# Graph attention on one core: GpSimd waits for the landing of one pair's gathers before it issues the next pair's

## The reference

```
q, k, v = x @ Wq + bq, x @ Wk + bk, x @ Wv + bv          # per node
e       = edge_attr @ We                                 # per edge
alpha   = sum_d(q[dst] * (k[src] + e)) / sqrt(16)        # per edge and head
attn    = softmax of alpha over the edges of one dst
out     = segment_sum(attn * (v[src] + e), dst)
x_r     = x @ Wskip + bskip
beta    = sigmoid([out, x_r, out - x_r] @ Wbeta)
out     = beta * x_r + (1 - beta) * out
out     = x + relu(layernorm(out) * gamma + beta_ln)
result  = layernorm(x + out)
```

## Time and profile before

| | |
|---|---|
| runs: median (lowest to highest) | 2126.05 us (2125.98 to 2133.83), 3 runs |
| profiled execution: span, first to last instruction | 2774.7 us |
| PE matmul busy in it | 2009.6 us, 72% |
| DVE busy | 1801.8 us, 65% |
| GpSimd busy | 1497.6 us, 54%, of it 1568 gathers 1483.1 us |
| ACT busy | 1140.6 us, 41% |
| DMA moved | 468.47 MB, GpSimd's queue 206.24 MB |
| mean granted TensorE clock | 0.77 |

### The profile page before, as it was taken

How to read it: one execution, slowest core, us unless ns; L and a number is a source line. 1 busy time by engine, 2 the same in 40 slices (tenths; PEclk the granted TensorE clock), 3 DMA queues, 4 the chain that set the end, 5 groups by cost and what they waited for, 6 DMA issues and landing times.

```text
span 2774.7 us, 45026 instructions
## 1 busy us (share of the span) xinstructions
PE 2009.6 (72%) x11492; PEld 1805.8 (65%) x11492; DVE 1801.8 (65%) x4040; ACT 1140.6 (41%) x3750; POOL 1497.6 (54%) x1591
## 2 busy tenths in 40 slices
PE   7478888888776577667766767757687777778775
PEld 5467777777666566566665767656576667667664
DVE  7465565566666566566665667657676676777764
ACT  0133333344343344344443444434454454454455
POOL 0555555555556555565555555555555555555531
PEclk9677777777777777777777777778788777777786
DMA  8556666666655555555554655555565555555541
GB/s 308 185 165 184 176 184 183 178 180 180 172 167 167 158 159 167 154 174 165 167 167 143 176 163 167 175 149 165 164 176 167 170 176 168 169 172 180 169 123 39
DMA packets 298585, 468.47 MB, mean 169 GB/s; under 512 B 49862, under 2 KB 193034, under 8 KB 298230
## 3 DMA queue, kind: packets, MB, share of 16 engines
q1 hardware_dynamic: 222680, 259.30, 31.3%
q0 software_dynamic: 75648, 206.24, 26.2%
HBM read 414.62 MB, written 50.73 MB: 168 GB/s over the span
## 4 chain that ended last, share of the span: by engine, by line
PE 54%; issue 17%; another core or an unknown queue 13%; ACT 8%; DVE 3%; DMA 2%; ACTq 1%; POOL 0%; SPq 0%; POOLq 0%; DVEq 0%
PE sum_ps L928 18%; PE q_ps L825 12%; PE e_ps L812 10%; ACT dist_en L1046 3%; PE max_ps L841 2%; PE sum_ps L866 2%; PE sum_ps L865 2%; PE sum_ps L851 2%; PE max_ps L834 2%; PE sum_ps L850 2%; ACT hot_en L1055 1%; PE sum_ps L894 1%; PE sum_ps L895 1%; DMA xt_buf<-xT 1%
## 5 line engine op out<-in xcount | busy, mean ns | idle before, releaser
L706 POOL DMA_INDIRECT kv<-kv_tab,src_all x1568 | 1483.1, 946 | 1144.6 <-DVE kve L1373 683.8
L1373 DVE TENSOR_TENSOR kve<-kv,e_ps 128x1024 f32<-128x1024 f32 x392 | 462.2, 1218 | 756.0 <-issue 626.2
L928 PE MATMUL sum_ps<-wv,hot_en 128*128 128x136 f32 x3136 | 683.7, 394 | 15.0 <-issue 11.4
L928 PEld LDWEIGHTS sum_ps<-wv,hot_en 128*128 128x128 f32 x3136 | 626.1, 291 | 60.4 <-issue 58.5
L825 PE MATMUL q_ps<-q_win,hot_ne 128*128 128x128 f32 x3136 | 458.8, 284 | 265.2 <-issue 262.8
L825 PEld LDWEIGHTS q_ps<-q_win,hot_ne 128*128 128x128 f32 x3136 | 401.5, 197 | 281.0 <-issue 278.1
L1046 ACT ACTIVATE dist_en<-iota_n,neg_rel 128x128 bf16<-128x128 f32 x1568 | 497.7, 389 | 75.9 <-issue 75.9
L812 PE MATMUL e_ps<-we,ea 128*128 128x128 f32 x3136 | 422.6, 292 | 13.1 <-issue 7.2
L1083 ACT COPY sums<-sum_ps 128x136 f32<-128x136 f32 x392 | 98.3, 263 | 798.5 <-remote 730.6
L812 PEld LDWEIGHTS e_ps<-we,ea 128*128 128x128 f32 x3136 | 415.3, 212 | 12.7 <-issue 6.4
L834 PE MATMUL max_ps<-ident,top 128*1 128x128 f32 x196 | 65.0, 332 | 332.8 <-ACT used_b L1060 296.5
(11 more groups left out here) (136 smaller groups left out, 1573.7 us busy)
## 6 DMA issues: line engine op xcount, KB each, us to landing
ea<-eaT SPq DMA_DIRECT2D x196, 512.0 KB
row_b<-rel_row SPq DMA_DIRECT2D x196, 256.0 KB
kv<-kv_tab,src_all POOLq DMA_INDIRECT x1568
q_win<-q_tab SPq DMA_DIRECT2D x392, 64.0 KB
sum_tab<-sums SPq DMA_DIRECT2D x392, 59.5 KB
kv_tab<-tab_buf SPq DMA_DIRECT2D x33, 384.0 KB, 3.7
logit<-sum_tab SPq DMA_DIRECT2D x49, 136.0 KB
xt_buf<-xT SPq DMA_DIRECT2D x33, 192.0 KB, 4.0
```

The source lines that it names most:

```text
L706: pool.indirect_dma_start(out=kv[:, s, t, :], out_offset=None, in_=kv_tab[:, :], in_offset=bass.IndirectOffsetOnAxis(ap=src_all[:, tile:ti ...
L928: mm = pe.matmul(sum_ps[u][:, 0:AC], hot_en[:, s, t, :], wv[:, s, t, :], start=(t == 0), stop=(t == TILES_G - 1))
L1373: dve.tensor_tensor(kve[:, s, :, :, :], kv[:, s, :, :].rearrange("p t (a c) -> p t a c", a=2), e4.to_broadcast([P, TILES_G, 2, C]), ALU.ad ...
```

## The change

Before the gathers of a pair are issued (all but the first pair's), GpSimd waits until the gathers of both slots of the pair in front have landed: `kv_ld` of the other parity's two slots must hold the full count.

```
 def gather(q):
     par = q % 2
+    if q:
+        for u in range(2):
+            pool.wait_ge(kv_ld[2 * (1 - par) + u], 16 * TILES_G * ((q - 1) // 2 + 1))
     for u in range(2):
         s = 2 * par + u
         if q >= 2:
```

## The result

The changed kernel takes 2824.95 us (2821.1 to 2830.8, four runs), the kernel before 2126.02 us (2125.94 to 2133.83, four runs): a ratio of 1.327, 95% interval 1.325 to 1.329. The direction is the forecast one. The size is not: +699 us instead of +404 us, and 2825 lies above the range of 2380 to 2690 us.

The account below looks back on a forecast made before the run. GpSimd's gather issue was taken as the bound: 9.70 us of issue, 2.10 landing and 0.27 start make 12.07 us a pair instead of 10.00, so 2126 + 404 = 2530 us; range 2380 to 2690 us.

Parts of the forecast that it names:

- GpSimd's issue bounds the timed kernel: GpSimd issuing 1568 gathers at a 1.25 us pitch, 10.00 us a pair, sets the timed kernel's 2126 us.
- (a): Timed GpSimd idles some 2 us a pair and the wait falls into it: nothing changes, 2126 us; chance 0.09.
- (b): Timed gathers issue at, say, 1.15 us pitch; another engine holds 10.00 us: wait partly absorbed, +267, 2393 us; chance 0.08.
- Rival (d): Pausing gathers lets the other engines run: faster, period of, say, 9.7 us, 58 us less, 2068 us; chance 0.03.
- the sum for the kernel before: First gather at 78.9 us, 195 pairs at 10.00 us, last issue 9.70, landing 1.85, tail 85.75: 2126.2 us.
- One pause a pair, from the end of the last issue to the landing, plus a start: Ahead of pairs 1 to 195: GpSimd's period becomes 12.07 us instead of 10.00, adding 404 us.
- The landing L: Time from the end of a pair's last gather issue to its landing: taken as 2.1 us, within 1.25 to 3.0.
- rival (c): Gathers land more slowly under load, near 3.0 us after the last issue throughout: 2705 us; chance 0.12.
- the "steady" 1.85 us: Landing time read in the profiled execution, from the last issue's end to `kve`'s start, with other engines silent: 1.85 us.
- the standstill: In the profiled execution the other engines stop while gathers are in flight; its end was read as the landing, covering the wait.
- The start after the wait: Delay before GpSimd's next gather once its wait is met: 0.27 us; the two added waits taken as free when met.
- The wait costs nothing where the kernel stands still, and the profiled span hardly moves: In the profiled execution the added wait is covered; its span stays near 2775 us, between 2750 and 2810 us.

Follow-up runs that it names:

- stand-in: Against the kernel before: two waits ahead of each pair, on the pair two in front, so always met when GpSimd comes to them; 2130.03 us, ratio 1.0001.
- the swap: Against the changed kernel: the same two waits ahead of each pair, the later slot named first; 2729.87 us, ratio 1.283 to the kernel before.

## Why the prediction was wrong in its size

**GpSimd's issue bounds the timed kernel: right.** The pitch of 1.25 us without a break stands in the stand-in's timeline, and taking a gather out takes time out. Rivals (a) and (b), some or no slack on GpSimd, are out. Rival (d) has nothing for it in the usual condition. That the sum for the kernel before met the median within 0.2 us was in part luck: the stand-in's first gather starts at 79.3 instead of 78.9 us, and behind its last issue come 85.9 us where the prediction had 87.6, with too short a landing and the tail of the other condition.

**One pause a pair, from the end of the last issue to the landing, plus a start: right.** By (2824.95 - 2126.02) / 195 the period is 13.58 us instead of 12.07. 9.70 us of issue stayed.

**The landing L, taken as 2.1 us: wrong, it is 3.05 us.** This is the step that failed first and the largest of three terms that were mis-sized. Against 2.1 us that is 0.95 us x 195 = 185 us. The row of the first pair under SP's loads, 2.97 us, which the prediction took as its upper end, was close to the usual value. But rival (c), at 0.12, had only this part: 2705 us. What went wrong is the weight given to the "steady" 1.85 us: it was read in a condition where all other engines stood still and SP issued nothing. That the end of the standstill was the landing is not shown either; in the next pair it ended 1.09 us after the last issue, and no landing read in the changed kernel is shorter than 1.74 us. The experiments show where 0.77 us of the difference comes from: the load of `row_b`, which SP issues just ahead of the last gathers. What is left between 2.24 and the 1.8 us of the quietest pairs was not taken out by any run. Loads of `ea` and `q_win` are not it. In the kernel with all three loads small, the 43 pairs in which SP issued a load for finished nodes between 1.5 us ahead of and 1.0 us behind the end of the last issue have a landing of 2.57 us in the mean, the other 152 one of 2.15. That points at these loads for a part; stores of sums and the gathers' own traffic remain.

**The start after the wait, taken as 0.27 us: wrong in this kernel, it is 0.71 us.** The 0.27 us were measured on a wait that stands in the gather's own instruction. The change brings three waits to the first gather, and the one that blocks went into an instruction of its own. That is 0.44 us x 195 = 85 us.

**A term that the sum did not have: 25 us.** The 14 gaps inside pairs are 2.05 us instead of 0.30. With them the three terms make up the missing 295 us (185 + 85 + 25). The gap depends on the place of the blocking wait as the start does: swapped, it is 0.55 us. So of the 95 us that the swap gave, the start explains 0.47 us x 195 = 92 and the gaps 21, and a landing longer by 0.09 us took some 18 back. That 92 and 95 agree so well is in part luck.

**The wait costs nothing where the kernel stands still, and the profiled span hardly moves: not tested.** The span did move little, from 2774.7 to 2821.8 us (2750 to 2810 was said), but that is luck: the two profiles are of different conditions, and the changed kernel was never met in the one of the first profile. The reading that the standstill belongs to one execution only was wrong: the kernel before took 2810 us in seven timed runs. What brings a chip into it, what holds the engines there, and why small loads are faster in it (2608 against 2669 us) stays open. Rival (d)'s thought, that a pause lets the others run, may hold there: the kernel that pauses and has small loads took 2608 us beside the kernel before's 2810.

## What to carry to other kernels

A wait that is put ahead of an issuing engine's work costs that engine the full way from its last issue to the landing, if the engine is the bound; behind a few more issues it costs nothing. Where the latency enters such a sum, take it from rows in which the other queues are as busy as they will be, and look at what is issued just ahead of the last transfer: here one such load cost 0.77 us a pair, and a larger one, issued earlier, nothing that could be measured. Where several waits meet at one instruction, name the one that will be late so that it is carried by the instruction itself (here: first), and check where it went: the trace lists the separate wait instruction with its duration.

## What was not expected of the hardware

- A blocking wait in an instruction of its own costs GpSimd 0.71 us from `kve`'s start at the landing to the next gather, one that the gather carries 0.24 us; of the waits here the one named first in the source was carried by the gather.
- With the blocking wait ahead of a pair, every thirteenth pair has a gap of 2.05 us behind its first gather (0.55 us where the gather carries the wait); in the stand-in, whose waits are met, there is none over 0.32 us. Its cause is open.
- Of 512 KB and 256 KB loaded in each pair, cutting the first by seven eighths gained nothing measurable and cutting the second 151 us. The second is issued 2.5 us ahead of the end of the last gather's issue, the first 7 us; the second cut also took packets away, the first did not.
- The same kernel took 2127 us and, in another set of seven runs on the same chip, 2810 us. In that set the kernel that pauses its gathers and has small loads took 2608 us, less than the kernel before.
